# A graph network's attention layer: node work of seven-tile groups moved into the pass over the edges, and a feed-forward pipeline of groups

## The reference, cut to what matters

```python
h = relu(layernorm(x))                       # input of layer 2
# layer 2: attention over edges and self-loops, 8 heads of 16
e = leaky(a_s[src] + a_d[dst]); m = segment_max(e, dst)
alpha = exp(e - m[dst]) / segment_sum(...)
gat = segment_sum(hW[src] * alpha, dst) + b_gat
h1 = layernorm(h + gat) * g1 + bb1           # first norm
ff = relu(h1 @ W1 + b1) @ W2 + b2            # 128 -> 512 -> 128
x = x + layernorm(h1 + ff) * g2 + bb2        # second norm
h = relu(layernorm(x))                       # third norm, input of layer 3
# layer 3: 10 steps y = 0.9 * A_norm y + 0.1 * h, then x = x + relu(y)
```

## Time and profile before

| | |
|---|---|
| median of 3 runs | 5615.09 us |
| profiled execution, its own time | 5616.37 us |
| its span, first to last instruction | 5614.6 us |
| attention pass, about 1893 to 2880 | 987 us |
| from there to the step loop, 2880 to 3183 | 303 us |
| mean granted TensorE clock | 0.90 |

### The profile page before, as it was taken

One profiled execution on the slowest core, in us unless ns is written; L12 is line 12 of the kernel. 1 busy time (PEld: TensorE's weight loads), 2 busy tenths in 40 slices (PEclk: granted clock), 3 DMA queues, 4 the chain that ended last, 5 costly groups with the idle time before them and its releaser, 6 DMA issues.

```text
span 5614.6 us, 96636 instructions
## 1 busy us (share of the span) xinstructions
PE 4488.0 (80%) x33763; PEld 3724.6 (66%) x33763; DVE 3023.1 (54%) x9553; ACT 1035.0 (18%) x2929; POOL 3214.8 (57%) x3380
## 2 busy tenths in 40 slices
PE   1888749999997356666537299999999999999997
PEld 1555536666665355555533288888888888888887
DVE  5888745555554566666683543434334343344434
ACT  3878631111112100000004300000000000000000
POOL 1000027777774577777720176766767667676765
PEclk8999979999998677767668699999999999999999
DMA  3111122222221343433410266666666666666656
GB/s 118 76 76 71 67 71 66 67 66 66 66 66 38 90 96 96 97 97 97 97 36 0 95 198 187 199 187 195 190 189 198 184 194 192 187 199 187 199 182 183
DMA packets 353713, 696.81 MB, mean 124 GB/s; under 512 B 98754, under 2 KB 233192, under 8 KB 352929
## 3 DMA queue, kind: packets, MB, share of 16 engines
q1 hardware_dynamic: 245552, 466.34, 26.1%
q0 software_dynamic: 107648, 223.88, 15.7%
HBM read 596.34 MB, written 93.92 MB: 123 GB/s over the span
## 4 chain that ended last, share of the span: by engine, by line
PE 41%; DVE 4%; POOL 3%; issue 2%; DMA 1%; ACT 1%; POOLq 0%; DVEq 0%; SPq 0%
PE ps L1469 23%; PE pt L1469 11%; PE pt L1487 5%; POOL E L803 1%; POOL arena L838 1%; PE ps L1431 1%; PE ps L1439 1%; ACT A L935 1%; DMA table<-E 0%; DMA arena<-x_spill,src_i 0%; DVE C L1635 0%; DMA arena<-table,src_i 0%; DVE E L1635 0%; PE pt L1196 0%; DVE B L2073 0%
## 5 line engine op out<-in xcount | busy, mean ns | idle before, releaser
L788 POOL DMA_INDIRECT arena<-table,src_i x782 | 742.5, 949 | 908.5 <-DMA table<-A 670.5
L838 POOL DMA_INDIRECT arena<-table,src_i x890 | 848.3, 953 | 670.7 <-DMA table<-E 400.9
L838 POOL DMA_INDIRECT arena<-x_spill,src_i x890 | 847.6, 952 | 345.4 <-issue 254.8
L803 POOL DMA_INDIRECT E<-gat_table,src_i x782 | 751.1, 960 | 340.2 <-issue 235.4
L1298 PE MATMUL ps<-E,arena 128*128 128x288 f32 (+7 forms) x3116 | 787.5, 405 | 96.6 <-DMA arena<-table,src_i 95.5
L1469 PE MATMUL ps<-E,arena 128*128 128x256 f16 x6370 | 726.6, 275 | 109.5 <-DVEq L2102 96.8
L1469 PEld LDWEIGHTS ps<-E,arena 128*128 128x128 fp8e4 x6370 | 627.7, 99 | 189.4 <-issue 111.6
L1469 PE MATMUL ps<-A,arena 128*128 128x256 f16 x6370 | 725.3, 275 | 0.2
L1298 PEld LDWEIGHTS ps<-E,arena 128*128 128x128 f32 x3116 | 505.2, 193 | 315.6 <-issue 144.7
L1469 PEld LDWEIGHTS ps<-A,arena 128*128 128x128 fp8e4 x6370 | 627.4, 99 | 78.5 <-issue 1.5
L2128 DVE SCALAR_TENSOR_TENSOR O<-ps,sc_b,O 128x128 f32<-128x128 f32 x260 | 91.2, 351 | 818.8 <-PE ps L1469 740.5
(11 more groups left out here) (317 smaller groups left out, 5516.9 us busy)
## 6 DMA issues: line engine op xcount, KB each, us to landing
arena<-adj SPq DMA_DIRECT2D x386, 784.0 KB
adj<-E SPq DMA_DIRECT2D x49, 784.0 KB, 3.3
arena<-table,src_i POOLq DMA_INDIRECT x1672
O<-dst_rows SPq DMA_DIRECT2D x112, 224.0 KB, 3.4
x_spill<-A SPq DMA_DIRECT2D x245, 64.0 KB
table<-E SPq DMA_DIRECT2D x245, 64.0 KB
arena<-x_spill,src_i POOLq DMA_INDIRECT x890
E<-gat_table,src_i POOLq DMA_INDIRECT x782, 3.8
```

The costliest lines, as they stand in the source:

```text
L788: pool.indirect_dma_start(out=rows_ring[:, k % RING, :], out_offset=None, in_=table, in_offset=bass.IndirectOffsetOnAxis(ap=src_i[:, k:k + ...
L803: pool.indirect_dma_start(out=att_rows[:, b % 3 * AB + at, :], out_offset=None, in_=gat_table, in_offset=bass.IndirectOffsetOnAxis(ap=src_ ...
L838: pool.indirect_dma_start(out=y_rows[:, g % ERING, k, :], out_offset=None, in_=(table, x_spill)[half], in_offset=bass.IndirectOffsetOnAxis ...
```

## The change

The residual (self-loop, mix, bias, residual) and the first norm of each group are cut into nine stages, and stage s of group r runs on its engine at the end of batch 8r + s (s from 10 to 18) of the attention pass, in `residual`. What lies beyond batch 55 runs after the pass: for group 5 its normalization and gain, for group 6 everything. The mask products of the branch that runs are left out, and the sum is made in C in place.

FF, second norm, third norm and state become one pipeline over the seven groups. PE works through a group's first product (8 pieces, L1431 before), the turn of the group two ahead, and the second product of the group before. The second product now takes the hidden tile as stationary operand and W2 as moving one, 28 matmuls of 128 columns to a group, so its result has nodes on the partitions and no transposes back are needed. ACT and DVE have the later stages of older groups behind their part of the present one; the root, the statistics and the halves of the state are made by groups. SP loads the adjacency tiles after the last second product, and stores the table in seven parts as their lower halves are done. The one-hot row `iota_y` is copied before the pass instead of after it. Some small buffers move.

```diff
+        RESIDUAL = {"self": 10, "exp": 11, "mix": 12, "sum": 13, "stats": 14, "root": 15, "stand": 16, "norm": 17, "gain": 18}
+        RESIDUAL_END = 8 * (PTN - 1) + RESIDUAL["gain"] + 1
+        def residual_at(v, stage):
+            r, late = divmod(v - RESIDUAL[stage], 8)
+            return r if late == 0 and 0 <= r < PTN else None
...
 # SP
-                    sp.wait_ge(sem("ffb"), PTN)
+                    sp.wait_ge(sem("ff2_ps"), PTN)
                     for u in range(ADJ_SLOTS):
                         load_adj(u, u)
-                    sp.wait_ge(sem("lower"), NT)
-                    sp.dma_start(table_v, nodes(E)).then_inc(sem("y_out0"), 16)
+                    for r in range(PTN):
+                        sp.wait_ge(sem("y_lower0"), r + 1)
+                        c = slice(r * T7, (r + 1) * T7)
+                        sp.dma_start(table_v[:, c, :], nodes(E)[:, c, :]).then_inc(sem("y_out0"), 16)
...
 # ACT, in the pass: residual(b) behind the copies of batch b; after it:
+                if b == 0:
+                    copy_h3T(0)
+                for v in range(ABATCHES + 1 if b == 0 else 0, RESIDUAL_END):
+                    residual(v)
+                copy_h3T(1)
+                for p in range(PTN + 7):
+                    if p < PTN:
+                        for g in range(8 * p, 8 * p + 8):
+                            h, c = g % 8 // 4, g % 4
+                            act.wait_ge(sem("ff1_ps"), g + 1)
+                            act.activation(ff1_out[p % 2][:, c, h * 448:(h + 1) * 448], ps[c % 2][:, 0:448],
+                                           ACT.Relu, bias=b1[:, c:c + 1]).then_inc(sem("ff1"), 1)
+                    if p + 2 < PTN:
+                        copy_h3T(p + 2)
+                    if 0 <= p - 2 < PTN:
+                        root_of("second", p - 2)
+                    if 0 <= p - 3 < PTN:
+                        norm_of("second", p - 3, C, B, ACT.Identity)
+                    if 0 <= p - 4 < PTN:
+                        root_of("third", p - 4)
+                    if 0 <= p - 5 < PTN:
+                        norm_of("third", p - 5, X, A, ACT.Relu)
+                    # and the upper half of group p - 6
...
 # PE
+                turn(0)
+                turn(1)
+                for p in range(PTN + 1):
+                    if p < PTN:
+                        pe.wait_ge(sem("h3T"), p + 1)
+                        # eight first products, each waits for the activation two before
+                    if p + 2 < PTN:
+                        turn(p + 2)
+                    if p:
+                        second_product(p - 1)
+                def second_product(r):
+                    pe.wait_ge(sem("ff1"), 8 * (r + 1))
+                    pe.wait_ge(sem("ff2"), r) if r else None
+                    for n in range(T7):
+                        for c in range(4):
+                            mm = pe.matmul(ps[2 + n // 4][:, n % 4 * P:(n % 4 + 1) * P],
+                                           ff1_out[r % 2][:, c, n * P:(n + 1) * P], w2[:, c, :],
+                                           start=(c == 0), stop=(c == 3))
+                    mm.then_inc(sem("ff2_ps"), 1)
...
 # DVE: mix, sum, stats in the pass
+                r = residual_at(v, "mix")
+                    link(dve.tensor_tensor(th(e2), agg[:, c, D:D + HEADS], th(self_w), ADD))
+                    link(dve.reciprocal(e2, e2))
+                    link(dve.tensor_tensor(heads(C[:, cf]), heads(C[:, cf]), bc(self_w, HC), MUL))
+                    link(dve.tensor_tensor(nodes(C)[:, c, :], nodes(C)[:, c, :], agg[:, c, 0:D], ADD))
+                r = residual_at(v, "sum")
+                    link(dve.tensor_tensor(heads(C[:, cf]), heads(C[:, cf]), bc(self_e[2], HC), MUL))
+                    link(dve.tensor_tensor(nodes(C)[:, c, :], nodes(C)[:, c, :], row_bc(rows[:, B_GAT, :], T7), ADD))
+                    link(dve.tensor_tensor(C[:, cf], C[:, cf], A[:, cf], ADD))
+                r = residual_at(v, "stats")
+                    moments(C, r, first_st, first_mv)
...
 # DVE, behind the pass
+                for step in range(PTN + 6):
+                    if step < PTN:
+                        added(step)               # 2 adds from PSUM, bias, moments
+                    if 0 <= step - 1 < PTN:
+                        standard("second", step - 1, scratch("second", step - 1)[1])
+                    if 0 <= step - 2 < PTN:
+                        second_out(step - 2)      # gain, shift, X, moments
+                    if 0 <= step - 3 < PTN:
+                        standard("third", step - 3, scratch("third", step - 3)[1])
+                    if 0 <= step - 4 < PTN:
+                        state_out(step - 4)       # two scalings
+                    if 0 <= step - 5 < PTN and b == 0:
+                        # lower half of group step - 5, then y_lower0
```

More of the change, by code:

```diff
@@ L48 @@
 BD, BK = 5, 26
+T7 = 7
+PTN = NT // T7
 NB = NT * BK
@@ L1044, in attention, with root_of, norm_of, residual @@
                     agg_out(b - 1, 1)
+                    residual(b)
+            def root_of(which, r):
+                act.wait_ge(sem("to_root"), 5 + ln_order.index((which, r)) + 1)
+                c = slice(r * T7, (r + 1) * T7)
+                act.activation(stat_b[:, c], stat_b[:, c], ACT.Sqrt).then_inc(sem("rooted"), 1)
+            def norm_of(which, r, x, h, function):
+                act.wait_ge(sem("norm_stats"), 3 + norm_order.index((which, r)) + 1)
+                for n in range(r * T7, (r + 1) * T7):
+                    act.activation(nodes(h)[:, n, :], nodes(x)[:, n, :], function,
+                                   bias=stat_a[:, n:n + 1], scale=stat_b[:, n:n + 1]).then_inc(sem("normalized"), 1)
+            def residual(v):
+                r = residual_at(v, "exp")
+                if r is not None:
+                    act.wait_ge(sem("self_exponents"), r + 1)
+                    act.activation(self_w, self_w, ACT.Exp).then_inc(sem("self_w"), 1)
+                r = residual_at(v, "root")
+                if r is not None:
+                    root_of("first", r)
+                r = residual_at(v, "norm")
+                if r is not None:
+                    norm_of("first", r, C, A, ACT.Identity)
+            def copy_h3T(r):
+                act.wait_ge(sem("h3T_ps"), r + 1)
+                act.activation(B[:, r * T7 * P:(r + 1) * T7 * P], pt[r % 2][:, 0:T7 * P], ACT.Copy
+                               ).then_inc(sem("h3T"), 1)
             def after_l1(b):
@@ L1076, in after_l2 @@
             def after_l2(b):
[L1077 to L1089, removed]
@@ L1422, in after_l2, with turn @@
             def after_l2(b):
[L1423 to L1426, removed]
-                        for c in range(4):
-                            g = 4 * n + c
+                def turn(r):
+                    pe.wait_ge(sem("ln_a"), r + 1)
+                    if r >= 2:
+                        pe.wait_ge(sem("h3T"), r - 1)
+                    for n in range(T7):
+                        i = r * T7 + n
+                        mm = pe.transpose(pt[r % 2][:, n * P:(n + 1) * P], A[:, i * P:(i + 1) * P], ident[:, :])
+                    mm.then_inc(sem("h3T_ps"), 1)
@@ L2085, in after_l2 @@
[L2085 to L2092 removed]
+                for v in range(ABATCHES if b == 0 else 0, RESIDUAL_END):
+                    residual(v, b)
@@ new lines, in second_out @@
+                def second_out(r):
+                    c, cf = group(r)
+                    dve.wait_ge(sem("normalized"), 3 * NT + T7 * (norm_order.index(("second", r)) + 1))
+                    link(dve.tensor_tensor(nodes(B)[:, c, :], nodes(B)[:, c, :], row_bc(rows[:, G2, :], T7), MUL))
+                    link(dve.tensor_tensor(nodes(B)[:, c, :], nodes(B)[:, c, :], row_bc(rows[:, BB2, :], T7), ADD))
+                    link(dve.tensor_tensor(X[:, cf], X[:, cf], B[:, cf], ADD))
+                    moments(X, r, *scratch("third", r))
```

204 lines of the change are left out of this document (128 added, 76 removed).

## The result

The changed kernel takes 5475.23 us (median of 4 runs, 5473.77 to 5477.46) against 5615.10: a ratio of 0.9752 (0.9740 to 0.9765), 139.9 us faster. The forecast was 5488, so the side and the range held; the size was 13 us short. The profiled execution has a span of 5471.9 us.

The account below looks back on a forecast made before the run. Gather instructions of POOL were taken to set the pass's pace, leaving DVE room, with 303 serial us behind it; stretch -132, pass +12 +2, first step -9, net -127 and -1.3 from 5616.4 give 5488 us, range 5470 to 5504 (0.70).

Parts of the forecast that it names:

- The stretch: From the last aggregated tile to the step loop: 23.4 + 93 + 54.5 = 170.9 us against 303, so -132.
- part 2: From the last aggregated tile to the first FF activation: serial for group 6, 23.4 us where it was 110.
- part 3: FF pipeline: three engines near 14 us a group, 93 us to the end of iteration 6, then 54.5 set by DVE.
- rival (a): FF pipeline slower: second product bound by 190 ns weight loads, +30, or engines waiting in a ring, +18; chance 0.14.
- last sign: FF pipeline: prediction falls if any engine idles much in each period with another pipeline engine as its releaser.
- The pass: Attention pass: +12 us for gathers slowed beside the residual's DVE instructions, +2 at its end.
- part 1: Residual and first norm inside the attention pass: fits DVE's spare time, costs gathers 12 us and the end +2.
- rival (b): Attention pass: POOL held up by the whole 44 us, +32, 5520; chance 0.09 with times between it and the forecast.
- Rival (c): Groups in the pass cost nothing and the first step gains its 11 us: 5474; within the forecast's chance of 0.70.
- Rival (d): In the pass DVE waits on ACT, some 17 waits of 17.65 us, up to 300 longer: 5788; chance 0.02.
- Rival (e): Stretch behind the pass stays serial; only the residual of six groups moves, about 58 us: 5557; chance 0.04.
- part 4: First step of the loop: table store mostly under the drain, last piece some 4 us instead of 13.6; -9 us.

Follow-up runs that it names:

- the second pair: Kernel before and changed kernel, each profiled again without edits on one chip: 5611.8 us and 5476.6 us.
- the pair with SBUF and PSUM: Changed kernel plus thirty large DVE instructions in the pass, second input from SBUF in one, PSUM in the other: 5482.2 and 5481.1 us.
- the old tail: Changed kernel with FF, norms, state and single table store as in the kernel before, on the slow chip: 6868.0 us.
- the residual behind the pass: Changed kernel with all nine residual and first-norm stages after the last batch, pipeline kept, on the slow chip: 6905.5 us, ratio 0.9942.

## Why the prediction was right

**What bounded the kernel.** Right at the usual speed, in both halves: DVE had the room in the pass, and the 303 us were serial. On the slow chip the first half is wrong: there POOL waits for DVE, and the gain is 112 us in place of 140.

**The stretch: 170.9 said, 162.8 measured**. To the first FF activation 19.2 instead of 23.4. This term of part 2 was mis-sized by its order: I had put the turn of group 0, its copy and group 6's self in line. The timeline shows self under ACT's copy and normalization (2.0), and the turn begun before the last node tile was copied, so that turn and copy cost 1.3 behind it and not 2.9 (1.6); the exponential ended before the gain did (0.35). From there to the end of iteration 6 it was 89.2 instead of 93: periods of 13.8 and 13.0 against 14.1 and 13.2, 8.0 for iteration 0 against 9.0, and almost no handovers. The drain took 54.45 against 54.5, and step by step too: 14.0, 13.9, 9.3, 9.0 and 8.2 for the rest, against 13.9, 13.9, 9.4, 9.1 and 8.2. In the FF itself the three engines are not all near 14, as part 3 has it: PE is, DVE reaches 12.5 and ACT 11.0 in the fullest period. The groups by form, 2860 to 3060, settle rival (a):

```profile
L1518 PE MATMUL ps<-B,w 128*128 128x448 f32 x112 | 50.0, 575 | 16.9 <-ACT arena L1142 16.6 <-ACT B L1093 0.2
L1503 PE MATMUL ps<-w,arena 128*128 128x128 f32 x392 | 45.0, 275 | 1.5 <-DVE C L2226 1.5
L1503 PEld LDWEIGHTS ps<-w,arena 128*128 128x128 f32 x392 | 44.5, 192 | 2.4 <-issue 2.4
```

A weight load has a record of 192 ns and a product one of 275, and still 392 of them take 45.0 us, 0.115 each: the records of neighbours overlap, loads and products alike (44.5 us busy in loads, 45.0 in products, in the same stretches). Choosing the row of a whole run (98 records in 11.21) over the mean of one record was right: the mean would have said 74. The ring of rival (a) isn't there either: in the whole FF PE waits 1.5 us for DVE. The prediction's last sign, that no engine of the pipeline should idle much for another in each period, was drawn too wide: ACT and DVE do wait for PE (28.0 and 43.0 us), and only PE's own waits bear on the period.

**The pass: +14 said, +7.3 measured** (+7.1 in the second pair). The gathers' part is the mis-sized term of part 1: the mechanism of the earlier trace rows is there, with 12 gathers over 1.2 us in place of 2, but the busy time of all grew by 4.5 us (5.8 in the second pair) and not by 12. What stands behind the last gather, the +2 of part 1, grew by 2.9 (1.2). The longest, in POOL's and DVE's timeline:

```profile
2253.74 1.12 POOL L824 DMA_INDIRECT E<-gat_table,src_i  x1 [0.30 <-issue]
...
2255.11 1.09 DVE L2090 TENSOR_TENSOR C<-C,w_tot 128x896 f32<-128x896 f32 x1
2255.17 1.85 POOL L824 DMA_INDIRECT E<-gat_table,src_i  x1 [0.30 <-issue]
2256.24 1.09 DVE L2091 TENSOR_TENSOR C<-C,arena 128x896 f32<-128x896 f32 x1
2257.32 0.94 POOL L824 DMA_INDIRECT E<-gat_table,src_i  x1 [0.31 <-issue]
```

The gather ends 0.8 us behind the end of the DVE instruction that started with it (2257.02 after 2256.20), as the one of 2.12 us above does (2315.52 after 2314.70, the end of the first of the three), and there the next gather runs its 0.94 although DVE works on. Of the 12 gathers over 1.2 us ten stand beside the residual's large instructions, of which some 40 fall before the last gather: one in four lengthens a gather by much. I had taken each gather that meets such an instruction to wait for the rest of it, for nearly all of it in a run of three. That overshot: a run mostly lengthens one gather and not the next. The plain scaling of the earlier trace rows (0.75 in 4.2 us), which gave 8 us, was nearer. The rule that the prediction cites from the Trainium skill (GPSIMD Engine Reference, section 1, Specifications) has its direction confirmed by the pair with SBUF and PSUM; of the 44 us of rival (b) 4.5 came. Rival (c), nothing at all, is for the gathers nearer than the forecast's 12. The last gather, expected 5 to 20 us after 2861, starts at 2856.7, as the pass began earlier; counted from the first gather it is 4.5 later. That the measured 5475 is rival (c)'s 5474 is luck: the pass did cost 7 us, the loop did not gain its 11, and the stretch made up for it.

**Rival (d)** did not occur: from 1880 to 2880 DVE waits for ACT once, 4.8 us at 2879.04 for the last node tile, and in none of the inserted stages. **Rival (e)** neither: the old tail and the residual behind the pass give the two parts at 55 and 83.

**The first step: -9 said; -6.1 and -11.0 measured, and given back.** The store lands 3.9 us after the last half and not 14, as part 4 has it. What the prediction lacked is the loop behind it: the nine later half pairs take 4.7 and 5.4 us more in the two pairs of profiles, so the loop as a whole gained 1.4 and 5.6. Part 4 as a term of the total is the one that failed: 7.6 and 3.4 us short of its 9. It is as large as the 8 us that the stretch gave over the sum and the 7 that the pass cost less, and runs the other way, so it hid part of their miss. That the forecast came within 13 us owes something to this.

No rival of the prediction had the gain taken back behind the first half pair.

Added up for the first pair: stretch -140.1, pass +7.3, loop -1.4, and the 8.5 us of scatter ahead of the pass make -142.7 between the spans. The second pair, on one chip, has -139.5, +7.1, -5.6 and +0.8, together -137.2.

## What to carry to other kernels

Take the cost of a product from a whole run of its kind (its length over its count) and not from the duration in one record of it or of its weight load. When work moves into a stage that another engine paces, look in the trace for the pacing engine's instructions beside moved ones that take both inputs from SBUF. Here thirty such instructions held the gathers up by 5 to 6 us in all, and as many with one input in PSUM by less than 1, so a home in PSUM for one input is worth having where it is free. A few microseconds gained at the start of a long loop that balances engines against transfers are worth nothing until the end of the loop shows them.

## What the runs showed of the hardware

One of the chips ran the kernels in 6783 to 6975 us in all of 43 runs, where the others took 5469 to 5629. Its mean granted clock was 0.83 and 0.84, against 0.90 and 0.91; a gather instruction was as long as elsewhere (970 ns against 966), but PE stood still 378 us in 495 places in front of the adjacency products, for which the profile names no releaser. The waits of the changed kernel there, PE, whole span:

```profile
PE ps L1549 <- issue: 378.2, 495, 3.5
```

What slows that chip was not looked into. The change gains less on it: a ratio of 0.983 against 0.975.

A gather beside DVE instructions on 128x896 with two SBUF inputs took up to 2.12 us in place of 0.94; beside the same instructions with one input in PSUM, and nothing else, it took 0.94 or 0.95 in all 28 cases.
